# Scores of a transformer layer from two 64-row halves of the TensorE array, and a new order of work

## The reference

```python
h = _layernorm(x, ln1_g, ln1_b)
x = _attention(h, h, sa_wq, sa_wk, sa_wv, sa_wo, sa_bo) + x
h = _layernorm(x, ln2_g, ln2_b)
x = _attention(h, cond_emb, ca_wq, ca_wk, ca_wv, ca_wo, ca_bo) + x
h = _layernorm(x, ln3_g, ln3_b)
p = h @ ff_w1 + ff_b1
a, gate = (p[..., :D_FF], p[..., D_FF:])
h = a * jax.nn.gelu(gate, approximate=False) @ ff_w2 + ff_b2
return h + x
```

## Time and profile before

| | us |
|---|---|
| median of 3 runs | 1859.13 |
| the runs | 1855.98, 1861.18, 1859.13 |
| the profiled execution | 1857.24 |
| its span, first to last instruction | 1855.5 |

### The profile page before, as it was taken

One profiled execution on the slowest core, in us unless ns is written; L12 is line 12 of the kernel. 1 busy time (PEld: TensorE's weight loads), 2 busy tenths in 40 slices (PEclk: granted clock), 3 DMA queues, 4 the chain that ended last, 5 costly groups with the idle time before them and its releaser, 6 DMA issues.

```text
span 1855.5 us, 41989 instructions
## 1 busy us (share of the span) xinstructions
PE 1763.7 (95%) x13824; PEld 1700.0 (92%) x13824; DVE 1410.3 (76%) x2651; ACT 1149.5 (62%) x3256; POOL 1016.5 (55%) x1727
## 2 busy tenths in 40 slices
PE   3999999999999999999999999999999998999998
PEld 3999999999999999999999999999999998888887
DVE  4877777877888787878778888878888887666664
ACT  3767667766777777767667777777767776121121
POOL 3677666655656665566666666555655565110110
PEclk8999999999999999999999999999999999999999
DMA  6566666665555555556666666665555553000100
GB/s 178 139 154 158 151 158 158 162 164 141 143 139 139 136 136 135 143 141 155 167 159 165 163 165 151 154 154 146 146 142 142 137 142 97 23 24 23 35 12 23
DMA packets 225623, 241.22 MB, mean 130 GB/s; under 512 B 68352, under 2 KB 190592, under 8 KB 225408
## 3 DMA queue, kind: packets, MB, share of 16 engines
q1 hardware_dynamic: 225408, 238.55, 52.1%
HBM read 58.08 MB, written 12.58 MB: 38 GB/s over the span
## 4 chain that ended last, share of the span: by engine, by line
PE 59%; DVE 10%; SPq 9%; DMA 8%; issue 7%; POOL 4%; ACT 2%; ACTq 0%; DVEq 0%; POOLq 0%
PE QKB L298 10%; PE PVB L347 7%; DMA RING<-RING 7%; PE PTB L271 6%; PE WOP L312 5%; PE VB L332 5%; PE S L259 5%; PE S L715 5%; PE PTB L715 5%; PE S L260 4%; SPq L913 4%; DVE PL L505 3%; SPq L915 3%; PE QKB L728 2%; PE VB L728 2%
## 5 line engine op out<-in xcount | busy, mean ns | idle before, releaser
L470 DVE TENSOR_REDUCE NM<-S 128x4 f32<-128x1024 f32 x256 | 313.4, 1224 | 232.0 <-PE S L260 229.9
L404 ACT ACTIVATE PT<-S,NM 128x256 f32<-128x256 f32 x1024 | 480.3, 486 | 14.4 <-DVE NM L470 14.4
L391 ACT ACTIVATE PH<-PTB 128x1024 fp32r<-128x1024 f32 x256 | 262.7, 1026 | 258.4 <-PE PTB L271 257.4
L505 DVE TENSOR_TENSOR PL<-PTB,PH 128x1024 fp32r<-128x1024 f32 x256 | 313.5, 1225 | 10.6 <-ACT PH L391 3.7
L384 ACT ACTIVATE ON<-PVB 64x256 f32<-64x256 f32 x512 | 193.9, 379 | 192.4 <-POOL OT L631 121.0
L259 PE MATMUL S<-RING 128*128 128x256 f32 x1024 | 267.8, 294 | 33.5 <-DMA RING<-RING 31.7
L271 PE MATMUL PTB<-IDN,PT 128*128 128x128 f32 x2048 | 265.3, 272 | 0.0
L607 POOL CAST VR<-VF 128x256 fp32r<-128x256 f32 x256 | 104.6, 408 | 283.2 <-DVE VF L512 282.2
L260 PE MATMUL S<-RING 128*128 128x256 f32 x1024 | 257.2, 283 | 0.0
L259 PEld LDWEIGHTS S<-RING 128*128 128x128 f32 x1024 | 195.0, 190 | 49.5 <-DMA RING<-RING 46.1
L495 DVE TENSOR_TENSOR ON<-PVB,ON 64x256 f32<-64x256 f32 x512 | 207.6, 405 | 34.7 <-ACT ON L384 31.2
(11 more groups left out here) (106 smaller groups left out, 3337.3 us busy)
## 6 DMA issues: line engine op xcount, KB each, us to landing
RING<-RING SPq DMA_DIRECT2D x512, 192.0 KB, 2.9
RING<-RING SPq DMA_DIRECT2D x512, 128.0 KB, 2.8
RB<-denominators SPq DMA_DIRECT2D x512, 64.0 KB, 2.6
out_dram<-XR SPq DMA_DIRECT2D x32, 256.0 KB, 3.0
XR<-in_x_dram SPq DMA_DIRECT2D x16, 256.0 KB, 3.4
denominators<-RDT SPq DMA_DIRECT2D x256, 16.0 KB
XR<-out_dram SPq DMA_DIRECT2D x16, 256.0 KB, 3.0
CX<-in_ctx_dram SPq DMA_DIRECT2D x16, 192.0 KB, 2.8
```

What stands on the lines that cost most here:

```text
L391: e.activation(PH[:, :], PTB[:, :, :].rearrange("p i n -> p (i n)"), ACT.Copy) \
L404: last = e.activation(PT[:, c % 2, j * S:(j + 1) * S], S1[:, i, qt * S:(qt + 1) * S], ACT.Exp, bias=NM[:, j:j + 1], accum_out=DEN[:, c % 2 ...
L470: e.tensor_reduce(NM[:, :].rearrange("p (i t) -> p i t", t=TT), S1[:, :, :].rearrange("p i (t s) -> p i t s", t=TT), AX.X, ALU.max, negate ...
L505: e.tensor_tensor(PL[:, :], PTB[:, :, :].rearrange("p i n -> p (i n)"), PH[:, :].bitcast(F32), ALU.subtract).then_inc(a.dve_pl, 1)
```

## The change

- Scores are taken from QKS in place. For each tile of queries and each of the three terms, one product for the head in rows 0 to 63 and one for the head in rows 64 to 127, alternating, each with 64 active rows and with an output bank of its own: 12 products a slot in place of 8. The ring, its memory and its four DMAs a slot go.
- PE's order in a slot: scores(c), transposes of h or context, QK(c+2), V(c+1), WO(c-4), transposes of the exponentials (c-1), PV(c-2). PV was (c-1). PH gets two buffers.
- ACT's order: ON(c-3), context or gain and bias, four exponentials, high part of Q and K, PH(c-1). DVE's order: maxima in two halves, PL(c-2) in two halves, ON add (c-3), V, reciprocal and transpose of pair c itself, low part of Q and K, the residual add, the layer-norm steps. The gain and bias steps are in slots 4 and 5 of a sequence, before in 3 and 4.
- The context is copied to HF by ACT and split by POOL (pool_split_ctx), before by ACT and DVE from PSUM.
- Start: the first weights are loaded and split in halves of 512 columns; the second halves are loaded in slots -2 to 0 and split on ACT and DVE in slots -1 to 1. The second transpose of the first sequence goes to PVB, so it waits for nobody. Small loads (gains of the later norms, biases), wo and the x of later sequences are issued later, in slots.
- End: slots 256 to 259 and feed-forward units 0 to 3 alternate on PE; the same on ACT (2 units) and DVE (3 units).

```diff
-        RING = sb("RING", [P, 5120], F32R)
+        QKS = sb("QKS", [P, 2, 4, S], F32R)
-        PH = sb("PH", [P, 2 * TT * S], F32R)
+        PH = sb("PH", [P, 2, 2 * TT * S], F32R)
...
+        def pe_scores(e, sl):
+            c = sl.c
+            if sl.has(c):
+                sl.wait(e, a.dve_lo, c + 1)
+                sl.wait(e, a.act_exp, 2 * c)
+                r = c % 2
+                for qt in range(TT):
+                    for j, (q, k) in enumerate(((QHI, KHI), (QHI, KLO), (QLO, KHI))):
+                        for i in range(2):
+                            last = e.matmul(S1[:, i, qt * S:(qt + 1) * S],
+                                            QKS[OWN[i], r, q, qt * P:(qt + 1) * P], QKS[OWN[i], r, k, :],
+                                            start=j == 0, stop=j == 2)
+                last.then_inc(a.pe_s, 1)
...
-            if sl.has(c):
-                await_ring(e, c)
-                for i in range(2):
-                    sl.wait(e, a.act_exp, 2 * c - 1 + i)
-                    for qt in range(TT):
-                        q = RX[:, c % 2, i, Q1, qt * P:(qt + 1) * P]
-                        o = S1[:, i, qt * S:(qt + 1) * S]
-                        e.matmul(o, q, RX[:, c % 2, i, K1, :], start=True, stop=False)
-                        last = e.matmul(o, q, RX[:, c % 2, i, K2, :], start=False, stop=True)
-                last.then_inc(a.pe_s, 1)
...
             if sl.has(c - 1):
                 s = c - 1
+                sl.wait(e, a.act_exp, 2 * s + 2)
+                for i in range(2):
+                    sl.wait(e, a.dve_pl, 2 * s + i - 1)
...
+            if sl.has(c - 2):
+                s = c - 2
                 sl.wait(e, a.pl_v, s - s % 2 + 2)
                 sl.wait(e, a.dve_ad, s)
+                sl.wait(e, a.act_ph, s + 1)
+                sl.wait(e, a.dve_pl, 2 * s + 2)
+                for j, part in enumerate((PH[:, s % 2, :], PL[:, :])):
...
                 sl.wait(e, a.pe_s, c + 1)
-                e.tensor_reduce(NM[:, :].rearrange("p (i t) -> p i t", t=TT),
-                                S1[:, :, :].rearrange("p i (t s) -> p i t s", t=TT),
-                                AX.X, ALU.max, negate=True).then_inc(a.dve_nm, 1)
+                sl.wait(e, a.act_exp, 2 * c)
+                for i in range(2):
+                    e.tensor_reduce(NM[:, i * TT:(i + 1) * TT], S1[:, i, :].rearrange("p (t s) -> p t s", t=TT),
+                                    AX.X, ALU.max, negate=True).then_inc(a.dve_nm, 1)
+            if sl.has(c - 2):
+                s = c - 2
+                sl.wait(e, a.act_ph, s + 1)
+                sl.wait(e, a.pe_pv, s)
+                for i in range(2):
+                    cols = slice(i * TT * S, (i + 1) * TT * S)
+                    e.tensor_tensor(PL[:, cols], PTB[:, i, :], PH[:, s % 2, cols].bitcast(F32),
+                                    ALU.subtract).then_inc(a.dve_pl, 1)
...
+        def pool_split_ctx(e, sl, n, k):
+            m, par = n - B, n % 2
+            e.wait_ge(a.act_cf, 2 * m + k + 1)
+            sl.wait(e, a.pe_v, PAIRS * (n - 1))
+            sl.wait(e, a.pe_qk, PAIRS * (n - 1))
+            f = HF[:, k * S:(k + 1) * S]
+            e.tensor_copy(CT[:, par, k, :], f).then_inc(a.pl_ch, 1)
...
+        def act_weights(e, n, half):
+            e.wait_ge(d_wA[NCH * half + n], 16)
+            e.activation(WA[:, n, 0, half * HC:(half + 1) * HC], raw(n, half), ACT.Copy,
+                         scale=SCALE if n < KD else 1.0).then_inc(s_whi, 1)
...
-            def copy_ring(k):
-                r, done = k % 2, d_dup[k % 2]
-                e.wait_ge(a.dve_lo, k + 1)
-                if k >= 2:
-                    e.wait_ge(a.pe_s, k - 1)
-                for i in range(2):
-                    e.dma_start(RX[OWN[i], r, i, :, :].bitcast(F32), QKS[OWN[i], r, 0:3, :].bitcast(F32)) \
-                        .then_inc(done, 16)
-                    e.dma_start(RX[OTHER[i], r, i, K1:Q1 + 1, :].bitcast(F32), QKS[OWN[i], r, 0:4:3, :].bitcast(F32)) \
-                        .then_inc(done, 16)
...
-            run_slots(-2, ATT + 1, ATT, lambda sl: pe_attention_slot(e, sl))
-            pe_ffn(e, zero_ffn)
-            pe_slot(e, Slot(ATT + 1, ATT))
-            pe_slot(e, Slot(ATT + 2, ATT))
-            pe_slot(e, Slot(ATT + 3, ATT))
-            ffn(e, pe_ffn, 1)
+            run_slots(-2, ATT, ATT, lambda sl: pe_attention_slot(e, sl))
+            for j in range(4):
+                pe_slot(e, Slot(ATT + j, ATT))
+                pe_ffn(e, Slot(j, FU, 2))
+            ffn(e, pe_ffn, 4)
```

More of the change, by code:

```diff
@@ L193, in __init__ @@
                 self.pl_or = sem("pl_or")
+                self.pl_ch = sem("pl_ch")
+                self.pl_ct = sem("pl_ct")
                 self.pl_hh = sem("pl_hh")
@@ L222, in block_kernel, with pe_h @@
         attentions = (Attention(0, WA), Attention(1, WB))
-        def pe_h(e, sl, n, k):
+        def pe_h(e, sl, n, k, bank=VB):
             sl.wait(e, a.dve_xn, n + 1)
-            sl.wait(e, a.act_hf, 2 * n + k)
+            if bank is VB:
+                if k == 0 and n >= B:
+                    e.wait_ge(a.act_cf, 2 * (n - B + 1))
+                else:
+                    sl.wait(e, a.act_hf, 2 * n + k)
             for t in range(TT):
-                last = e.transpose(VB[:, S + t * P:S + (t + 1) * P],
+                last = e.transpose(bank[:, S + t * P:S + (t + 1) * P],
                                    XN[:, t * D + k * P:t * D + (k + 1) * P], IDN[:, :])
@@ L300, in pe_slot @@
                 last.then_inc(a.pe_qk, 1)
+            if sl.has(c + 1):
+                v = c + 1
+                n, p = divmod(v, PAIRS)
+                t = v % 2
+                sl.wait(e, a.dve_vf, v)
+                if prepares and pair in (1, 2) and seq + 1 >= B:
+                    sl.wait(e, a.act_cf, 2 * (seq + 1 - B) + pair)
+                if prepares and pair in (4, 5):
+                    sl.wait(e, a.act_hf, 2 * (seq + 1) + pair - 3)
+                if v == 0:
+                    e.wait_ge(a.act_hf, 2)
+                if v == 0 or v == HALF:
+                    e.wait_ge(s_wlo, NCH if v == 0 else 2 * NCH)
+                passes = list(attentions[n // B].kv_passes(4, n % 2))
+                for j, (w, act) in enumerate(passes):
+                    last = e.matmul(VB[:, 0:S], act[:, t * P:(t + 1) * P], w[:, (p - t) * P:(p - t + 2) * P],
+                                    start=j == 0, stop=j == len(passes) - 1)
+                last.then_inc(a.pe_v, 1)
             if sl.has(c - 4):
@@ L315, in pe_slot @@
                 last.then_inc(a.pe_wo, 1)
[L317 to L334, removed]
@@ L338, in pe_slot @@
+                last.then_inc(a.pe_t, 1)
+            if sl.has(c - 2):
+                s = c - 2
                 sl.wait(e, a.pl_v, s - s % 2 + 2)
                 sl.wait(e, a.dve_ad, s)
[L340 to L344, removed]
+                sl.wait(e, a.act_ph, s + 1)
+                sl.wait(e, a.dve_pl, 2 * s + 2)
+                for j, part in enumerate((PH[:, s % 2, :], PL[:, :])):
@@ L389, in act_slot @@
                 sl.wait(e, a.pe_t, s + 1)
-                sl.wait(e, a.pe_pv, s)
-                e.activation(PH[:, :], PTB[:, :, :].rearrange("p i n -> p (i n)"), ACT.Copy) \
+                sl.wait(e, a.pe_pv, s - 1)
+                e.activation(PH[:, s % 2, :], PTB[:, :, :].rearrange("p i n -> p (i n)"), ACT.Copy) \
                     .then_inc(a.act_ph, 1)
[L394 to L418, removed]
-                e.activation(QKS[:, k % 2, 0:2, :], QKB[:, :].rearrange("p (u s) -> p u s", u=2), ACT.Copy) \
-                    .then_inc(a.act_hi, 1)
-            if sl.has(c):
-                exponentials(1)
         def dve_stats(e, sl, a, n):
@@ new lines, in dve_slot @@
+            if sl.has(c - 3):
+                s = c - 3
+                sl.wait(e, a.act_lp, s + 1)
+                for i in range(2):
+                    on = ON[OWN[i], s % 2, :]
+                    last = e.tensor_tensor(on, PVB[OWN[i], i * S:(i + 1) * S], on, ALU.add)
+                last.then_inc(a.dve_ad, 1)
+            if sl.has(c + 1):
+                v = c + 1
+                sl.wait(e, a.pe_v, v + 1)
+                sl.wait(e, a.pl_v, v)
+                e.tensor_copy(VF[:, :], VB[:, 0:S]).then_inc(a.dve_vf, 1)
@@ new lines, in dve_slot @@
+            if sl.has(c):
+                sl.wait(e, a.act_exp, 2 * c + 2)
+                if c > 1:
+                    e.wait_ge(d_ds[(c - 2) % 4], 16 * ((c - 2) // 4 + 1))
+                e.reciprocal(RDEN[:, 0:4], DEN[:, c % 2, :]).then_inc(a.dve_rc, 1)
+                sl.wait(e, a.dve_rc, c + 1)
+                e.transpose(RDT[:, c % 2, :], RDEN[:, :]).then_inc(a.dve_rt, 1)
+            if sl.has(c + 2):
+                k = c + 2
+                sl.wait(e, a.act_hi, k + 1)
+                e.tensor_tensor(QKS[:, k % 2, 2:4, :], QKB[:, :].rearrange("p (u s) -> p u s", u=2),
```

(6 more changed lines are left out.)

304 lines of the change are left out of this document (156 added, 148 removed).

## The result

The changed kernel takes 1813.58 us (median of 4 runs, 1813.21 to 1815.46); the kernel before, on the same chip, 1860.16. The ratio is 0.9754, 95% interval [0.974, 0.9769]: 47 us faster, where 95 from the median of before were forecast. The time lies in the stated range of 1695 to 1890 and outside the 1740 to 1790 of the likeliest case.

A forecast was written before the change was run, and what follows sets the result against it. PE's own work was taken to set the slot (5.67 us in self-attention, 5.43 in cross-attention), with 90 us of stalls in attention. 1857.24 - 61 (1) + 51 (2) - 65 (3, 4) - 14 (5) - 4 (6) = 1764 us; range 1695 to 1890.

The forecast's parts named there:

- the likeliest case: Whole kernel: full pairing, 0.10 us a switch and most stalls gone, 1764 us; chance 0.31.
- Step 2: PE's switches between 128-row and 64-row products, 510 in attention: 0.10 us each, +51 us.
- the bare load (0.11): At a switch on PE: the next load isn't made ahead, 0.11 us, read from a restart row.
- the wait for the product before (0.16): At a switch on PE: the array must empty first, 0.16 us; rival at 1795 us, chance 0.15.
- The 0.27: At a switch on PE: drain and bare load together, the upper end; rival at 1851 us, chance 0.07.
- Step 1: PE's score products: six side-by-side pairs take 0.72 us against 0.96, -0.24 a slot, -61 us.
- The rival with 1.31 a block: PE's score block: loads of the two halves take turns, 1.31 us and not 0.72, 1914 us; chance 0.20.
- Steps 3 and 4: Attention slots: ring removed and engines reordered; 65 us of stalls go and 25 stay.
- the 90 us of old stalls: PE in attention before the change: 1526.0 us less 1436 of its own work, 0.35 a slot.
- Step 5: Kernel start: no ring wait and fewer weight splits ahead of Q and K(0), -14 us.
- Step 6: Kernel end: feed-forward units between the last slots fill PE's waits, -4 us.

The follow-up runs named there:

- experiment 1: Changed kernel with six 128-row score products a slot in place of twelve of 64 rows, some terms left out (scores changed): 1757.15 us, ratio 0.9472.
- experiment 4: Changed kernel with V's products put between the score products of the two query tiles in half of the slots: 1916.83 us, ratio 1.0333.
- Experiment 5: Changed kernel with GpSimd's rstd and context split moved behind ON and OT in slots 1 and 2 of a sequence: 1782.53 us, ratio 0.9579.
- experiment 8: Kernel before with its eight 128-row score products read in place from QKS, without the ring (scores changed): 1815.47 us, ratio 0.9751.
- experiment 2: Changed kernel with eight 128-row score products a slot in place of twelve of 64 rows (scores changed): 1802.22 us, ratio 0.9715.
- experiment 3: Changed kernel with all six 64-row score products of the first head ahead of the second head's six: 1889.82 us, ratio 1.0187.

## Why the prediction was off

**Step 2, the switches, is the step that failed, by size.** I took 0.10 a switch, 51 us; it is 0.19, so 0.37 to 0.38 a slot and about 96 us, shown by 5.79 against 5.42 in experiment 1 and by the 0.38 of experiment 4. With it the sum is 1809. I had both parts among my bounds, the bare load (0.11) and the wait for the product before (0.16), and took one of them; both occur. The 0.27 that I gave for both together was too much, since the wait is 0.09. The changed kernel's rows show them at the way in; rows of one block from overlapping windows, first PE, then the loads.

```profile
708.48 0.28 PE L353 MATMUL PVB<-PL,VR 128*128 128x256 f32 x1
708.69 0.39 PE L259 MATMUL S<-QKS 64*128 64x256 f32 x2
...
708.91 0.51 PE L259 MATMUL S<-QKS 64*128 64x256 f32 x5
709.03 0.52 PE L259 MATMUL S<-QKS 64*128 64x256 f32 x6
```

```profile
708.36 0.19 PEld L353 LDWEIGHTS PVB<-PL,VR 128*128 128x128 f32 x1
708.69 0.18 PEld L259 LDWEIGHTS S<-QKS 64*128 64x128 f32 x2
```

The last PV to the first pair: 0.21 in place of 0.12. The first pair to the second: 0.22. Then 0.12 a pair. The first loads of 64 rows start with their products (708.69) and not 0.12 ahead of them, and the first products' rows last 0.38 us, as the one behind the restart in rows 2 does. The way out, in a block of another slot:

```profile
745.74 0.28 PE L259 MATMUL S<-QKS 64*128 64x256 f32 x2
745.95 0.50 PE L293 MATMUL QKB<-HT,WA 128*128 128x256 f32 x2
```

The last pair to the first of Q and K is 0.21 again, and the second of these starts at 746.17 (745.95 + 0.50 - 0.28), 0.22 behind the first. The 0.19 is measured; that it is a wait and then a bare load is my reading of these starts. A switch of tiling mode drains the engine, says the Trainium skill's TensorEngine Tiling (Array Packing) (Tiling Modes). The trace agrees in that each switch holds PE up, by 0.09 us and not by my 0.16 for that rule; it doesn't show an empty array, for the next product starts 0.07 before the row of the last one ends (708.48 + 0.28).

**Step 1 was right:** both products of a pair start within 0.01 us, pairs 0.12 apart; no load takes turns. The rival with 1.31 a block falls.

**Steps 3 and 4, the stalls,** gave 57 of the 65: PE's work in the changed attention is 128 x 5.79 + 127 x 5.55 + 94 x 0.19 for the transposes = 1464, of 1497.2, so 33 are stalls, 25 forecast. That the two numbers are near is luck. Experiment 5 takes 30.3 of the 33 away by POOL's order alone, so of the 90 us of old stalls nearly all went, where I had let 25 stay without naming them, and about 30 new ones came. What I missed is POOL's queue: I priced the context's split as two more instructions on an engine with room and did not ask what waits behind rstd. The ring's part in attention, 34.1 in experiment 8, is what PEld's row gives without the first slot (46.1 - 10.7 = 35.4); PE's row, 21, is too low. And PV's wait for DVE's add isn't in my step; it decides in cross-attention once the switches are gone, where PE's own work from Q and K to PV is 22 x 0.12 + 0.79 = 3.43 and PV comes 3.55 behind (1185.12 to 1188.67 in experiment 1).

**Step 5** -15 against -14. Q and K(0) start at 11.50, 4.5 sooner, and the ring's wait went. A part of the agreement is chance: in the eight profiles with this start the first scores come at 18.1 to 19.9 us. The twelve products of Q and K(1) at 15.81 took 1.70 us in the changed kernel's profile and 2.93 in that of experiment 2, which started them at 15.68.

**Step 6** 0 against -4: the old waits went, and one for DVE's split ahead of unit 0 came.

Together, from rows: 0.12 x 255 = 31 for the longer slots, -3 for the transposes of rows and context, -57 stalls, -15 start, 0 end, -44 in all, as the spans have it (1855.5 to 1811.9).

## What to carry to other kernels

Price a change of the array's shape twice: the wait for the last product and the load that isn't made ahead, on the way in and out. Pairs of 64-row products pay only in blocks long enough: here six pairs save 0.24 us, 0.04 each, and the switches lose 0.38, so I estimate that some ten pairs a block would be needed. That holds against the ring, which gives three terms in two products. Against one full-height product for each 64-row one a pair saves 0.12, and by the same estimate four pairs would do. When an order is rewritten, list for every instruction that waits what is queued behind it, on the engines with room too: this gave 31 us here.

## What the runs showed of the hardware

- Products on rows 0 to 63 and 64 to 127 run side by side with their loads: 12 starts in 0.70 us, where 128-row products take 0.12 each.
- A switch between 64 and 128 rows costs 0.09 us before the next product and 0.10 before the second one; the latter is about 0.05 where transposes of 128 columns follow (0.165 apart for 0.11 usually). Two more switches in a slot cost 0.38 together (experiment 4).
- With the two heads not alternating, three of twelve products still started with the one before (experiment 3).
